# Row maxima by small transfers, four column tiles for the value products, residual in PSUM, routing in groups, another order

## The reference

```
x = layernorm(x + attn(x, x, causal), ln1)                 # 16 heads of 8 features
x = layernorm(x + attn(x, encoder_output), ln2)            # 77 keys
x = layernorm(x + moe(x), ln3)

def attn(q_in, kv_in):
    scores = (q_in @ wq + bq) . (kv_in @ wk + bk) / sqrt(8)   # causal: -inf above the diagonal
    return softmax(scores) @ (kv_in @ wv + bv) @ wo + bo

def moe(x):
    p = softmax(x @ rw + rb); two largest of 8, softmax over these two -> gates
    out = sum over both experts of gate * (gelu(x @ w1[e] + b1[e]) @ w2[e] + b2[e])
```

## Time and profile before

| | |
|---|---|
| median of 3 runs | 497.91 us (495.34 to 503.47) |
| profiled execution | 495.67 us, span 493.6 us |
| mean granted clock of TensorE | 0.916 |
| PE busy | 371.7 us, 75% |
| DVE busy | 315.4 us, 64% |
| ACT busy | 282.0 us, 57% |
| POOL busy | 171.4 us, 35% |

### The profile page before, as it was taken

How to read it: one execution, slowest core, us unless ns; L and a number is a source line. 1 busy time by engine, 2 the same in 40 slices (tenths; PEclk the granted TensorE clock), 3 DMA queues, 4 the chain that set the end, 5 groups by cost and what they waited for, 6 DMA issues and landing times.

```text
span 493.6 us, 8885 instructions
## 1 busy us (share of the span) xinstructions
PE 371.7 (75%) x2121; PEld 248.6 (50%) x2121; DVE 315.4 (64%) x1061; ACT 282.0 (57%) x648; POOL 171.4 (35%) x217
## 2 busy tenths in 40 slices
PE   2358779989988989999889997767603999999300
PEld 1323455565465465465465453353303999999300
DVE  9732555778778778778777877554371555555292
ACT  2017259679679679679679679516311555555132
POOL 9403112131441441431431432502120455554343
PEclk9999889999999999999999999965955999999855
DMA  8230302521341341350340340040872122221142
GB/s 223 82 74 0 71 16 49 140 51 29 84 131 30 82 134 28 82 141 19 88 131 24 88 138 12 24 137 18 259 184 52 42 70 64 60 62 51 55 124 85
DMA packets 38602, 39.92 MB, mean 81 GB/s; under 512 B 4762, under 2 KB 32271, under 8 KB 38552
## 3 DMA queue, kind: packets, MB, share of 16 engines
q1 hardware_dynamic: 36280, 35.11, 27.1%
q0 software_dynamic: 2272, 4.24, 2.5%
HBM read 13.66 MB, written 14.79 MB: 58 GB/s over the span
## 4 chain that ended last, share of the span: by engine, by line
PE 31%; DVE 25%; issue 11%; ACT 7%; DVEq 7%; DMA 7%; SPq 5%; POOL 3%; POOLq 0%; ACTq 0%
PE bank L535 6%; PE bank L479 4%; PE bank L522 4%; SPq L366 4%; DVEq L980 4%; PE bank L480 3%; DMA sa_km<-sa_ku 3%; ACT sa_qm L674 3%; PE bank L503 3%; DVE ca_nm L810 3%; DVE ca_us L983 2%; PE bank L502 2%; DVE yb L993 2%; PE bank L546 2%; ACT ca_qm L674 2%
## 5 line engine op out<-in xcount | busy, mean ns | idle before, releaser
L733 ACT ACTIVATE sa_us<-bank,expert_b 128x128 f32<-128x128 f32 x156 | 44.9, 367 | 48.8 <-PE bank L617 39.9
L1051 POOL TENSOR_SCALAR_AFFINE_SELECT sa_pt<-sa_pt 128x512 f32<-128x512 f32 x64 | 39.0, 635 | 71.5 <-ACT sa_pt L682 71.3
L1083 POOL DMA_INDIRECT results<-sa_us,xs x39 | 41.0, 1052 | 51.9 <-DVE sa_us L995 44.8
L810 DVE TENSOR_REDUCE sa_nm<-bank 128x4 f32<-128x512 f32 x64 | 41.6, 684 | 16.7 <-PE bank L503 16.5
L1074 POOL DMA_INDIRECT dispatched<-r_sent,r_row x32 | 31.8, 994 | 44.0 <-DVE r_sent L936 36.6
L617 PE MATMUL bank<-xsT,ca_us 128*128 128x128 f32 x312 | 45.2, 290 | 2.2 <-DVE ca_us L983 1.6
L674 ACT CAST sa_qm<-bank 8x512 fp32r<-8x512 f32 x64 | 36.9, 576 | 14.0 <-PE bank L510 12.4
L628 PE MATMUL bank<-ca_pt,sa_us 128*128 x312 | 43.8, 284 | 0.1
L674 ACT CAST ca_qm<-bank 8x512 fp32r<-8x512 f32 x64 | 36.8, 575 | 10.4 <-PE bank L510 9.2
L617 PEld LDWEIGHTS bank<-xsT,ca_us 128*128 128x128 f32 x312 | 39.4, 198 | 4.9 <-issue 3.1
L682 ACT ACTIVATE sa_pt<-bank 128x512 f32<-128x512 f32 x64 | 34.8, 597 | 10.4 <-PE bank L522 10.4
(11 more groups left out here) (210 smaller groups left out, 851.9 us busy)
## 6 DMA issues: line engine op xcount, KB each, us to landing
dispatched<-filler SPq DMA_DIRECT2D x17, 520.0 KB, 4.4
sa_km<-sa_ku SPq DMA_DIRECT2D x32, 96.0 KB
sa_qm<-sa_qu SPq DMA_DIRECT2D x32, 96.0 KB
ca_qm<-ca_qu SPq DMA_DIRECT2D x32, 96.0 KB
xs<-dispatched SPq DMA_DIRECT2D x39, 65.0 KB
sa_pt<-in_e_w SPq DMA_DIRECT2D x8, 256.0 KB, 5.2
ca_pt<-in_e_w SPq DMA_DIRECT2D x8, 256.0 KB, 6.1
sa_pt<-results SPq DMA_DIRECT2D x8, 256.0 KB, 4.7
```

The lines of the kernel that those rows point to most:

```text
L733: act.activation(hid[b][:, c, :], bank[2 * b + c // 2][:, P * (c % 2):P * (c % 2) + P], ACT.Gelu, bias=b1[:, bass.ds(expert * FC + c, 1)]) ...
L810: dve.tensor_reduce(k.nm[:, u, g, :], bank[home[k, "scores", u][g % 2]][:, :].rearrange("q (j n) -> q j n", j=J)[:, :, 0:k.keys], AX.X, AL ...
L1051: pool.affine_select(out=blockg, in_=blockg, compare_op=ALU.is_ge, fill=0.0, base=0, pattern=[[0, J], [1, P]], channel_multiplier=-1).then ...
L1083: pool.indirect_dma_start(out=results, out_offset=bass.IndirectOffsetOnAxis(ap=xs[v][:, P:P + 1].bitcast(I32), axis=0), in_=ys[v], in_offs ...
```

## The change

- `shift`: ACT makes one copy of the turned maxima into SBUF (`mT`), and SP writes them into the free rows of `qm` with four transfers of 8 rows, the source repeated for the four groups.
- The key copies take all 32 rows of a block instead of 24.
- `mix`: one product for each head, 32 stationary columns (8 values, a one, zeros) by 128 queries, into a column tile of 32 rows. A unit fills one bank instead of two, so one ACT copy and four transposes a unit instead of two and eight; DVE divides once a unit.
- `norm` works on a pair: PE adds the residual (and CA's output bias) in PSUM by products with the identity; DVE reads PSUM, and writes the new residual itself.
- Routing in groups: pairs (0, 1), (2, 3, 4), (5, 6), (7). The logits are still made pair by pair; the 27 other operations, the ranks and the dispatch run once a group, at its last pair. `fill` moves from the pair of lag 1 to lag 2.
- A new order and new banks.

```diff
+def routed_together(pairs):
+    groups, left = [], list(range(pairs))
+    for size in (2, 3, 2):
+        if len(left) > size:
+            groups.append(tuple(left[:size]))
+            left = left[size:]
+    return groups + [(p,) for p in left]
...
-            k.vo = t("vo", [keys, 2, GROUPS, 64])
+            k.vo = t("vo", [keys, 2, HEADS, 32])
+            k.mT = t("mT", [P, 2, P], F32R)
-            k.us = [t(f"us{u}", [P, 2, 512]) for u in range(2)]
+            k.us = [t(f"us{u}", [P, 512]) for u in range(2)]
...
         ORDER = [
-            (SA, "scores", 2, 0), (CA, "turn_heads", 1, -2), (CA, "spread_terms", 0, -1), (CA, "spread_terms", 1, -1),
...
+            (CA, 'restore', 1, -2), (SA, 'scores', 0, 0), (CA, 'mix', 2, -2), (SA, 'scores', 1, 0),
...
                 for j in range(J):
-                    rows = slice(32 * j + 8, 32 * j + 32)
-                    sp.dma_start(k.km[rows, j, 0:GROUPS * 2 * k.keys].bitcast(F32), k.ku[rows, :, :].rearrange("r g n -> r (g n)").bitcast(F32)).then_inc(k.s_bdk, 16)
+                    whole = slice(32 * j, 32 * j + 32)
+                    sp.dma_start(k.km[whole, j, 0:GROUPS * 2 * k.keys].bitcast(F32), k.ku[whole, :, :].rearrange("r g n -> r (g n)").bitcast(F32)).then_inc(k.s_bdk, 16)
...
+            def shift(k, p, u):
+                if not after_pair(p):
+                    sp.wait_ge(k.s_zero, 2)
+                sp.wait_ge(k.s_sha, p * 2 + u + 1)
+                if after_pair(p):
+                    sp.wait_ge(k.s_s2_ps, (p - 1) * 8 + 4 * u + 4)
+                for j in range(J):
+                    rows = slice(32 * j, 32 * j + 8)
+                    sp.dma_start(k.qm[rows, j, :, P * u:P * u + P].bitcast(F32),
+                                 k.mT[rows, u, :].bitcast(F32).rearrange("r (o n) -> r o n", o=1).to_broadcast([8, GROUPS, P])).then_inc(k.s_max[u], 16)
...
             def weights(k, p, part):
                 u, half = divmod(part, 2)
-                pe.wait_ge(k.s_sha, p * 8 + 4 * u + 4)
+                if half == 0:
+                    pe.wait_ge(k.s_max[u], p * 64 + 64)
...
                 for g in (2 * half, 2 * half + 1):
-                    b = home[k, "mix", u][g // 2]
                     pe.wait_ge(k.s_pm if k.causal else k.s_ex, p * 8 + 4 * u + g + 1)
-                    ins = pe.matmul(bank[b][64 * (g % 2):64 * (g % 2) + 64, :], k.vo[:, u, g, :], k.pt[u][:, 512 * g:512 * g + 512], start=True, stop=True)
+                    for j in range(J):
+                        ins = pe.matmul(bank[b][32 * j:32 * j + 32, P * g:P * g + P], k.vo[:, u, J * g + j, :],
+                                        k.pt[u][:, 512 * g + P * j:512 * g + P * j + P], start=True, stop=True)
...
             def norm(k, p, u):
-                pe.matmul(bank[home[k, "norm", u][0]][:, 0:D], k.oT[:, u, :], k.wo[:, :], start=True, stop=True).then_inc(k.s_w_ps, 1)
+                both = bank[home[k, "norm", u][0]][:, 0:2 * D].rearrange("q (v d) -> q v d", v=2)
+                pe.matmul(both, ident, residual[:, 2 * p:2 * p + 2, :], start=True, stop=False)
+                if not k.causal:
+                    pe.matmul(both, ident, k.bo.rearrange("q (o d) -> q o d", o=1).to_broadcast([P, 2, D]), start=False, stop=False)
+                for v in range(2):
+                    pe.wait_ge(k.s_ot, p * 2 + v + 1)
+                    ins = pe.matmul(both[:, v], k.oT[:, v, :], k.wo[:, :], start=False, stop=(v == 1))
...
             def shift(k, p, u):
-                for j in range(J):
-                    rows = slice(32 * j, 32 * j + 8)
-                    src = bank[home[k, "shift", u][0]][rows, 0:P].rearrange("r (o n) -> r o n", o=1).to_broadcast([8, GROUPS, P])
-                    act.copy(k.qm[rows, j, :, P * u:P * u + P], src).then_inc(k.s_sha, 1)
+                    act.wait_ge(k.s_max[u], p * 64)
+                act.copy(k.mT[:, u, :], bank[home[k, "shift", u][0]][:, 0:P]).then_inc(k.s_sha, 1)
...
             def norm(k, p, u):
-                pool.tensor_tensor(k.rs[:, u:u + 1], k.ba[:, u, 1:2], half[:, :], ALU.pow).then_inc(k.s_rs, 1)
-                    pool.tensor_copy(residual[:, bass.ds(p * 2 + u, 1), :].rearrange("q o d -> q (o d)"), k.x1[:, u, :]).then_inc(k.s_xr, 1)
+                pool.tensor_tensor(k.rs[:, :], k.ba[:, :, 1], half[:, :].to_broadcast([P, 2]), ALU.pow).then_inc(k.s_rs, 1)
             def number(k, p, u):
+                n, group = group_of[p]
+                if p != group[-1]:
+                    return
```

More of the change, by code:

```diff
@@ L78, in build @@
     PAIRS = B // 2
+    ROUTED = routed_together(PAIRS)
+    TILES = 2 * max(len(g) for g in ROUTED)
+    group_of = {p: (n, g) for n, g in enumerate(ROUTED) for p in g}
     SCALE = float(HD) ** -0.5
@@ L190, in kind @@
             k.s_sha = sem(f"{name}_sha")
+            k.s_max = [sem(f"{name}_max{u}") for u in range(2)]
             k.s_s2_ps = sem(f"{name}_s2_ps")
@@ new lines, in build @@
+            (CA, 'mix', 3, -2), (CA, 'turn', 0, -1), (SA, 'shift', 0, 0), (CA, 'project', 0, -1),
+            (CA, 'restore', 3, -2), (CA, 'turn_heads', 0, -2), (CA, 'spread_terms', 0, -1),
+            (CA, 'spread_terms', 1, -1), (SA, 'scores', 2, 0), (CA, 'turn_heads', 1, -2), (CA, 'norm', 0, -2),
+            (SA, 'scores', 3, 0), (RT, 'route', 0, -2), (RT, 'gate', 0, -2), (SA, 'shift', 1, 0),
+            (RT, 'choose', 0, -2), (CA, 'scores', 0, -1), (SA, 'weights', 0, 0), (SA, 'weights', 1, 0),
@@ L427, in _ @@
             held = {}
+            filling = set()
             def take(b):
+                assert b not in filling, b
                 for made, value in held.get(b, ()):
@@ L585, in place @@
-                ins = pe.matmul(dst, ones_bf[:, :], r.acc[:, :, :].rearrange("q v e -> q (v e)"), start=False, stop=True)
+                n, group = group_of[p]
+                if p != group[-1]:
+                    return
+                tiles = 2 * len(group)
+                pe.wait_ge(r.s_rt, n * ROUTER_OPS + SELECTED)
+                take(home[k, "place", u][0])
+                dst = bank[home[k, "place", u][0]][:, 0:tiles * EXPERTS].rearrange("q (v e) -> q v e", v=tiles)
+                for c in range(TOPK):
+                    ins = pe.matmul(dst, triangle_bf[:, :], r.chosen[:, c, 0:tiles, :], start=(c == 0), stop=False)
@@ L586, in place @@
+                for m in range(n):
+                    pe.matmul(dst, ones[:, :], r.total[:, m:m + 1, :].to_broadcast([P, tiles, EXPERTS]), start=False, stop=False)
+                for v in range(tiles - 1):
+                    for c in range(TOPK):
+                        last = v == tiles - 2 and c == TOPK - 1
+                        ins = pe.matmul(dst[:, v + 1:tiles, :], ones_bf[:, :], r.chosen[:, c, v:v + 1, :].to_broadcast([P, tiles - 1 - v, EXPERTS]), start=False, stop=last)
                 ins.then_inc(r.s_rank_ps, 1)
-                give(home[k, "place", u][0], r.s_rt, p * ROUTER_OPS + SELECTED + 6)
+                give(home[k, "place", u][0], r.s_rt, n * ROUTER_OPS + RANKED + 1)
@@ new lines, in place @@
+                if p != group[-1]:
+                    return
+                t = 2 * len(group)
+                if group[0]:
+                    dve.wait_ge(r.s_disp, group[0] * 64)
+                dve.wait_ge(r.s_exp, n * 2 + 2)
+                routed(p, dve.tensor_scalar(r.den[:, 0:t], r.ed[:, 0:t], 1.0, None, ALU.add))
+                gates = [r.sent[:, 0:t, c, ROW - 1] for c in range(TOPK)]
+                routed(p, dve.reciprocal(gates[0], r.den[:, 0:t]))
+                routed(p, dve.tensor_tensor(gates[1], r.ed[:, 0:t], gates[0], ALU.mult))
```

362 lines of the change are left out of this document (180 added, 182 removed).

## The result

The change makes the kernel slower: 510.94 us (median; 509.66 to 511.64) against 496.62 us (493.90 to 503.47), a ratio of 1.030 with a 95% interval of 1.025 to 1.036. The forecast was 460 us.

The account below looks back on a forecast made before the run. No engine full: PE's own work and short returns to ACT and DVE make the 36.5 us period. Less 5.2 us over about 7.3 periods: 495.7 - 38 + 1.5 + 2 - 1 = 460 us, forecast 445 to 478 (range 436 to 488).

Parts of the forecast that it names:

- period of 31.3 us: Repeating attention part: 36.5 us less 3.2 of PE work and 2.0 of waits, 5.2 us less.
- 0.60 forecast: Value products on PE: a half unit takes 0.60 us instead of 0.92, saving 2.6 us a period.
- this floor: Value products on PE: sequencer spends about 62 ns on each matmul, 0.99 us a half; sum near 482 us.
- -3.2 forecast: PE's work per period: value products and transposes save 2.6 and 1.9 us, identity products add 1.3.
- -2.0 of waits for ACT and DVE: PE's waits per period: 3.0 of 4.5 us go, the second unit's maxima take 1.0 back.
- DVE, per period: Normalising heads -1.4 us, residual add -1.1, grouped routing -3.6; net -6.1 us.
- I add 2 us once: POOL's dispatch: twelve indirect transfers, up to 16 us in a row, delay the norm's next power; +2 us.
- a loss of 1.5: Start of attention: the first iteration has nothing to hide the transfers, +1.5 us.
- -1: End of attention: the last routing has five operations fewer, -1 us.
- The slower rival: SP's queue becomes the path, 2.6 us a unit shown to PE: 536 us, chance 0.07; about half, 478 to 500, 0.09.
- Packing of records: Value products on PE: matmul records don't pack, a half takes 1.12 us; 491 us, chance 0.14.

Follow-up runs that it names:

- e5_order: Changed kernel with two self-attention weights steps and cross-attention's scores 0 placed around the second shift, route, gate and choose behind them: 530.4 us.
- e10_norm_later: Changed kernel with scores 3, weights 0 and shift 1 of self-attention ahead of cross-attention's norm, weights 1 and later steps behind it: 531.4 us.
- e17_fill_half: Changed kernel with three extra PE products ahead of route's wait and two ahead of the second self-attention unit's maxima: 506.9 us.
- e9_old_order: All parts of the change in the order and banks of the kernel before: 569.2 us, 1.154.
- e4_act: Changed kernel with the row maxima written into the query operand by ACT again, four copies a unit, no SP transfers of them: 570.0 us, 1.157.
- e7_mix2: Changed kernel with every value product issued twice into the same place: 535.2 us.
- e6_runs2: Changed kernel with a POOL pause of four waited-for memory fills after every two dispatch transfers: 499.0 us, 1.011 of the kernel before.
- e8_before_transfers: Kernel before, own order kept, with only the row maxima written by one ACT copy and four SP transfers a unit: 558.1 us, 1.128.
- e1_single: Changed kernel with every pair routed by itself, four dispatch transfers at a time: 511.7 and 516.8 us (all four: 511.69 to 520.86).

## Why the prediction was wrong

It forecast 460 us, from a period of 31.3 us, and almost every size of work in it was near. Two steps failed: the waits, and POOL's bursts.

**Right: the work.** Four column tiles do run side by side. A half unit's sixteen records start within 0.37 us, and the next product starts 0.58 us behind the first (0.60 forecast); before it was 0.92. The Trainium skill, "TensorE: Matmul & The Clock Gate", section "Wait — 56ns, not 53.3ns?", would have made it 0.99 us with hardware decode off. No row tells how the products were decoded; the 0.58 us say that this floor did not bind here. The rows of the three engines' new work, 122 to 157.4 us:

```profile
L564 PE MATMUL bank<-ca_pt,ca_vo 77*32 77x128 f32 x64 | 2.6, 279 | 0.0
L564 PE MATMUL bank<-sa_pt,sa_vo 128*32 128x128 f32 x64 | 2.4, 277 | 0.0
...
L736 ACT COPY sa_us<-bank 128x512 f32<-128x512 f32 x2 | 1.2, 586 | 2.1 <-PE bank L564 2.1
```

PE's work fell from 33.26 to 30.30 us, with the half clock in it (-3.2 forecast, -3.0 measured). ACT went to 18.6 (18), DVE to 24.3 us with a group's routing in the period and 20.6 in one without (23). A set of four maxima transfers issues in 2.98 us (2.8). Only the 32-row key copies missed: 2.47 us a set, not 1.9; the 0.43 us of a small load was no model for them. No end of the sum hangs on it.

**Wrong: "-2.0 of waits for ACT and DVE".** The sum took the period of the old order, subtracted work, and let waits shrink because ACT loses a third of its load. The text called this a choice, not a reading. Measured, the waits of a quiet period rose from 3.2 to 5.05 us, where the sum has 1.2: 3.8 us a period, some 28 us in 7.3 periods. Of the 5.05 us 2.9 stand at one place: `route` close behind the norm of a pair, and the maxima behind both. The prediction followed the transfers of the maxima through the new order and found them covered, which was right; it did not follow the norm, which a part of the change had just made into one round of DVE, POOL and DVE for two sequences. The step "DVE, per period" counted the residual add as a saving of 1.1 us and never asked who waits for the norm. That this round is what keeps the period long is not shown: the two orders that moved its users (e5_order, e10_norm_later) were slower, and filling the waits (e17_fill_half) changed the period by 0.1 to 0.7 us.

Behind that stands a larger fault. A period of 36.5 us was taken as PE's work plus small returns, from which parts can be subtracted. e9_old_order shows that the parts in the old order cost 75 us; e4_act shows that in the new one 8 us of ACT's work at one place pass on whole, and e7_mix2 that most of 3.5 us of PE's do. This fits a period that is a closed chain through several engines in program order, where work counts by its place in the chain and not by its engine's load. Two orders tried by hand both lost 20 us; whether another gains is open. Which chain closes at 35.4 us was not settled: e17_fill_half shows that PE's clock at the idle place adds at most 0.7 us to it.

**Wrong: "I add 2 us once" for POOL's bursts.** The place was named, the mechanism was not: the step had POOL's own queue, the norm's power behind the transfers. In the change the power comes 10 us after POOL is free (182.56, [10.09 <-DVE]). What counts is the hold of PE's signals, 11.9 us by e6_runs2. The kernel before has at most 1.1 us of it in a run of four, and none in two of seven, so its trace gave little warning.

**The rest of the loss.** With the pauses, 217.5 us for six periods against 218.2 is a gain of 0.7 and the start gains 3.1, where the forecast had a loss of 1.5; the two stretches behind the periods lose 4.5 and 2.9 us. A likely reason, not tested, is that there the last pairs have no other pair's work to lie beside, and that a group of three and a group of two are routed and sent in them. The forecast had "-1" for the last routing.

**The rivals.** The slower rival had the wrong place. SP's queue as the path is real in the old order (e8_before_transfers, +64 us), and in the new one it is covered. Packing of records, the rival with the most chance, was false.

## What to carry to other kernels

When a change brings its own order, a sum of savings made in the old one says little: here the same parts cost 75 us in one order and 14 in the other. Each new round trip has to be followed to whoever waits for it, in the new order, and an engine that is idle 40% of the time is no reserve unless the place is known. A step that is made for two units at once saves instructions, but its first user waits for both units. Ask of each batched step what its result's first user now stands behind, and of batched transfers how long they run without a break.

## What the runs showed of the hardware

- While POOL sends indirect transfers one after another (1.26 us apart), semaphore updates of PE can come late. In the changed kernel those of products that ended from 3.2 us after the first transfer on came from 5.8 us on in a run of four (five of e1_single's), 7.2 in one of eight, 10.0 in one of twelve, with further gaps of 1.4 to 2.1 us behind the first release in the two longer ones. In the kernel before a run of four made none over 1.1 us late. Updates of DVE in the same stretches came on time. With a break of 1.7 us after every two transfers those from 3.2 us on came within 0.05 us at the place of the run of eight, and the time was 11.9 us less; with one of 3.2 us after every four 7.4 less.
- Four 32-column products side by side start 7 ns apart, and four such sets follow each other 0.11 us apart, for 128 moving columns of fp32 in two records each.
- A transfer from 8 rows of SBUF to 8 rows, 4x128 elements each, takes SP 0.69 us to issue (median; up to 0.94), one of 32 rows of 1024 elements 0.59 us, one of 24 rows of 1024 elements 0.71 to 0.74 us (medians of the two kernels).
